# Mixture of experts: weights of the first experts loaded ahead into room that is free until later

## What is computed

```
x = x + 0.5 * ffn(layernorm(x))
x = x + attn(layernorm(x))
x = x + 0.5 * ffn(layernorm(x))

def ffn(h):                                 # E = 64 experts, 2 of them for each token
    x = rmsnorm(h) * rms_w
    topk_w, topk_ids = top_k(softmax(x @ gate_w.T), 2)
    xb = up to 256 of the tokens that chose expert e, for each e
    g, u = split(xb @ w13[e])               # w13[e]: 256 x 256 (256 KB)
    yb = (silu(g) * u) @ w2[e]              # w2[e]: 128 x 256 (128 KB)
    return weighted sum of a token's two yb rows + shared expert + h
```

## Time and profile before

| | us |
|---|---|
| median of three runs | 2201.7 (2197.7 to 2204.65) |
| the profiled execution | 2191.9 |
| its span, first to last instruction | 2189.4 |

### The profile page before, as it was taken

How to read it: one execution, slowest core, us unless ns; L and a number is a source line. 1 busy time by engine, 2 the same in 40 slices (tenths; PEclk the granted TensorE clock), 3 DMA queues, 4 the chain that set the end, 5 groups by cost and what they waited for, 6 DMA issues and landing times.

```text
span 2189.4 us, 32445 instructions
## 1 busy us (share of the span) xinstructions
PE 1970.7 (90%) x11044; PEld 1670.2 (76%) x11044; DVE 1310.7 (60%) x3467; ACT 1087.5 (50%) x1988; POOL 1116.0 (51%) x1252
## 2 busy tenths in 40 slices
PE   6996989499999999999999999999999973988887
PEld 4665888478888888888888888888888862888754
DVE  5995565445566566575576575575565452554467
ACT  6873666344445345444454454454454432555643
POOL 6785676444254555545545645645625325665500
PEclk9998999799999999999999999999999985999999
DMA  8434888790032032032031110110100202888778
GB/s 277 157 115 152 270 285 282 253 287 20 1 97 78 20 96 78 20 97 68 30 96 38 60 51 25 41 43 17 58 10 20 87 17 67 286 274 290 238 253 278
DMA packets 236407, 270.07 MB, mean 123 GB/s; under 512 B 25490, under 2 KB 186323, under 8 KB 236243
## 3 DMA queue, kind: packets, MB, share of 16 engines
q1 hardware_dynamic: 199122, 192.40, 27.4%
q0 software_dynamic: 28672, 67.22, 9.4%
q10 hardware_dynamic: 8448, 8.39, 1.1%
HBM read 150.35 MB, written 117.57 MB: 122 GB/s over the span
## 4 chain that ended last, share of the span: by engine, by line
PE 59%; DVE 8%; issue 5%; ACT 4%; POOL 2%; another core or an unknown queue 1%; DMA 1%; SPq 0%; ACTq 0%; DVEq 0%; POOLq 0%
PE attention_ring L1925 20%; PE attention_acc L1955 13%; PE attention_acc L1945 8%; DVE attention_hid_l L1658 2%; PE attention_work L1998 2%; PE attention_work L2031 2%; PE attention_work L2035 2%; PE attention_work L2015 2%; PE attention_acc L2138 2%; PE attention_ring L2164 2%; PE attention_acc L2128 1%; PE attention_work L1913 1%; PE attention_ring L2128 1%; PE attention_work L1972 1%
## 5 line engine op out<-in xcount | busy, mean ns | idle before, releaser
L1658 DVE TENSOR_TENSOR attention_hid_l<-attention_gelu,attention_hid_h 128x512 fp32r<-128x512 f32 x384 | 284.8, 742 | 495.4 <-ACT attention_gelu L1302 311.8
L1299 ACT ACTIVATE attention_hid_h<-attention_ring,home_b 128x512 fp32r<-128x512 f32 x384 | 264.2, 688 | 565.2 <-PE attention_ring L1925 488.8
L1302 ACT ACTIVATE attention_gelu<-attention_ring,home_b 128x512 f32<-128x512 f32 x384 | 261.7, 681 | 0.0
L1955 PE MATMUL attention_acc<-attention_hid_h,home_w_h 128*128 128x512 f32 x512 | 202.6, 396 | 20.8 <-DVE home_room L1684 18.0
L1925 PE MATMUL attention_ring<-attention_n_t_h,home_w_h 128*128 128x512 f32 x512 | 204.8, 400 | 1.4 <-DVE attention_n_t_l L1650 1.4
L1925 PE MATMUL attention_ring<-attention_n_t_h,home_w_l 128*128 128x512 f32 x512 | 200.6, 392 | 0.0
L1925 PE MATMUL attention_ring<-attention_n_t_l,home_w_h 128*128 128x512 f32 x512 | 200.2, 391 | 0.0
L1955 PE MATMUL attention_acc<-attention_hid_l,home_w_h 128*128 128x512 f32 x512 | 199.5, 390 | 0.0
L1955 PE MATMUL attention_acc<-attention_hid_h,home_w_l 128*128 128x512 f32 x512 | 199.4, 389 | 0.0
L1146 POOL DMA_INDIRECT home_room<-expert_rows,routing_slots x128 | 138.0, 1078 | 96.9 <-issue 52.7
L647 POOL DMA_INDIRECT experts_xg<-xn_rows,routing_affine x128 | 142.6, 1114 | 67.9 <-issue 35.2
(11 more groups left out here) (279 smaller groups left out, 5233.5 us busy)
## 6 DMA issues: line engine op xcount, KB each, us to landing
experts_w<-in_L_ffn_w SPq DMA_DIRECT2D x64, 256.0 KB
expert_rows<-experts_y SPq DMA_DIRECT2D x64, 256.0 KB
slot_rows<-const_zeros SPq DMA_DIRECT2D x16, 1024.0 KB
token_rows<-const_zeros SPq DMA_DIRECT2D x16, 1024.0 KB
home_room<-in_L_ffn_w SPq DMA_DIRECT2D x64, 256.0 KB
home_room<-slot_rows SPq DMA_DIRECT2D x64, 256.0 KB
final_y_rows<-token_rows SPq DMA_DIRECT2D x32, 512.0 KB, 6.7
dispatch_x_in<-in_L_attn_x SPq DMA_DIRECT2D x16, 512.0 KB, 6.5
```

Of the source, the lines that this page charges most:

```text
L1299: act.activation(hid[n % PARTS][0][:, :], ring[n % RING][:, :], ACT.Gelu, bias=b1[:, m, c:c + 1])
L1302: act.activation(gelu[n % GELUS][:, :], ring[n % RING][:, :], ACT.Gelu, bias=b1[:, m, c:c + 1]).then_inc(ring_free, 1)
L1658: dve.tensor_tensor(hid[n % PARTS][1][:, :], gelu[n % GELUS][:, :], hid[n % PARTS][0][:, :].bitcast(fp32), ALU.subtract).then_inc(hid_read ...
L1955: last = pe.matmul(acc[e % 3][:, :], w2[m][wp][:, c, k * P:(k + 1) * P], hid[s][xp][:, :], start=(c == 0 and q == 0), stop=(c == FC - 1 an ...
```

## The change

The weights of the first ten experts (FIRST = 10) go to tiles of their own, `home.first_w13` and `home.first_w2`, which lie over the last four of the twelve split attention weights (`h2_w2` and `fm_w2`, made after experts 31 and 47). For this the split weights get a fixed place at the upper end of SBUF, also during the dispatch. They are loaded in the dispatch by two DMAs (2.6 MB and 1.3 MB), which SP issues after `store_xn(10)` and so ahead of `store_base(8)`; nothing in the dispatch waits for them.

In the experts, SP first loads experts 10 to 13 into the ring. Experts 14 to 23 go again to the room of the first ten, in two lots of five (`load_again`, one DMA of 1.3 MB and one of 0.66 MB each), issued after the stores of experts 4 and 9. Experts 24 to 27 go to the ring one by one at e = 14, 16, 18 and 20, and from e = 24 on expert e + 4 is loaded as before. An expert's `w13` and `w2` share one semaphore now, and both `round_weights` and `down` wait until both have landed (`weights_in`); before, `round_weights` waited for `w13` alone.

```diff
                 store_xn(g)
                 if g + RX < GROUPS:
                     load_x(g + RX)
+                if g == GROUPS - RX:
+                    home.load_first(sp, w)
                 if g >= 2:
                     store_base(g - 2)
...
-        w13_loaded = [sem(f"w13_loaded{s}") for s in range(R)]
-        w2_loaded = [sem(f"w2_loaded{s}") for s in range(R)]
+        w_loaded, again_loaded = [sem(f"w_loaded{s}") for s in range(R)], [sem(f"again_loaded{n}") for n in range(2)]
...
+        FIRST, HALF = home.FIRST, home.FIRST // 2
+        AHEAD = FIRST + R
+        RING_AGAIN = AHEAD + FIRST
+        def held(e):
+            return e < FIRST or AHEAD <= e < RING_AGAIN
+        def slot_of(e):
+            return e % AHEAD if held(e) else (e - FIRST if e < AHEAD else e - RING_AGAIN) % R
+        def weights_in(e):
+            if e < FIRST:
+                return home.first_loaded, 32
+            if held(e):
+                return again_loaded[(e - AHEAD) // HALF], 32
+            return w_loaded[slot_of(e)], 32 * (1 if e < AHEAD else 2 + (e - RING_AGAIN) // R)
...
+            def load_again(n):
+                first, at = AHEAD + n * HALF, slice(n * HALF, (n + 1) * HALF)
+                sp.wait_ge(w_split, (n + 1) * HALF)
+                sp.dma_start(home.first_w13[:, at, :], w["w13"][first:first + HALF, :, :].rearrange("e (p k) f -> p e (k f)", k=KD)).then_inc(again_loaded[n], 16)
+                sp.wait_ge(y_ready, (n + 1) * HALF)
+                sp.dma_start(home.first_w2[:, at, :], w["w2"][first:first + HALF, :, :].rearrange("e p d -> p e d")).then_inc(again_loaded[n], 16)
...
-            for e in range(R):
+            for e in range(FIRST, AHEAD):
                 load_w13(e)
                 load_w2(e)
...
             for e in range(EXPERTS):
-                if e + R < EXPERTS:
+                if e in (HALF, 2 * HALF):
+                    load_again(e // HALF - 1)
+                if AHEAD <= e < AHEAD + 2 * R and e % 2 == 0:
+                    load_w13(RING_AGAIN + (e - AHEAD) // 2)
+                    load_w2(RING_AGAIN + (e - AHEAD) // 2)
+                if e >= RING_AGAIN and e + R < EXPERTS:
                     load_w13(e + R)
                     load_w2(e + R)
                 store(e)
...
             def round_weights(e):
-                act.wait_ge(w13_loaded[e % R], 16 * (e // R + 1))
+                act.wait_ge(*weights_in(e))
...
             def down(e):
                 pe.wait_ge(hidden_ready, e + 1)
-                pe.wait_ge(w2_loaded[e % R], 16 * (e // R + 1))
+                pe.wait_ge(*weights_in(e))
```

More of the change, by code:

```diff
@@ L654, in round_weights @@
             def round_weights(e):
[L655 removed]
+                act.wait_ge(*weights_in(e))
                 if e >= F:
                     act.wait_ge(gate_up_ready, e - F + 1)
[L658 removed]
+                act.activation(w13_hi[e % F][:, :, :], w13_of(e), ACT.Copy).then_inc(w_rounded, 1)
             def round_rows(e):
@@ L702, in split_weights @@
                     dve.wait_ge(gate_up_ready, e - F + 1)
-                dve.tensor_tensor(w13_lo[e % F][:, :, :], w13[e % R][:, :, :], w13_hi[e % F][:, :, :].bitcast(fp32), ALU.subtract).then_inc(w_split, 1)
+                dve.tensor_tensor(w13_lo[e % F][:, :, :], w13_of(e), w13_hi[e % F][:, :, :].bitcast(fp32), ALU.subtract).then_inc(w_split, 1)
             def split_rows(e):
@@ L762, in down @@
                 for c in range(CH):
-                    last = pe.matmul(ps_y[e % F][:, c, :], hidden[e % F][:, c * P:(c + 1) * P], w2[e % R][:, :], start=True, stop=True)
+                    last = pe.matmul(ps_y[e % F][:, c, :], hidden[e % F][:, c * P:(c + 1) * P], w2_of(e), start=True, stop=True)
                 last.then_inc(y_ready, 1)
@@ L806, in load, with load_first @@
             sp.dma_start(row[:, :], w[name].partition_broadcast(P)).then_inc(self.b_loaded, 16)
+    def load_first(self, sp, w):
+        sp.dma_start(self.first_w13[:, :, :], w["w13"][0:self.FIRST, :, :].rearrange("e (p k) f -> p e (k f)", k=KD)).then_inc(self.first_loaded, 16)
+        sp.dma_start(self.first_w2[:, :, :], w["w2"][0:self.FIRST, :, :].rearrange("e p d -> p e d")).then_inc(self.first_loaded, 16)
     def make_weights(self):
-        fr = mybir.dt.float32r
-        self.weights_at = -(-self.kit.nc.sbuf_base // 32) * 32
-        self.w1 = [[self.kit.sb(f"w1_{m}_{part}", [P, KD, 1024], fr) for part in "hl"] for m in range(3)]
-        self.w2 = [[self.kit.sb(f"w2_{m}_{part}", [P, 1024 // P, D], fr) for part in "hl"] for m in range(3)]
+        fr, at, size = mybir.dt.float32r, self.weights_at, 8192
+        place = self.kit.nc.alloc_sbuf_tensor_at
+        self.w1 = [[place(f"w1_{m}_{part}", [P, KD, 1024], fr, offset=at + (2 * m + n) * size) for n, part in enumerate("hl")] for m in range(3)]
+        self.w2 = [[place(f"w2_{m}_{part}", [P, 1024 // P, D], fr, offset=at + (6 + 2 * m + n) * size) for n, part in enumerate("hl")] for m in range(3)]
     def part(self, n, p):
```

22 lines of the change are left out of this document (15 added, 7 removed).

## The result

| | before | after |
|---|---|---|
| median of five runs, us | 2201.7 (2197.7 to 2204.65) | 2214.2 (2212.1 to 2221.2) |
| the profiled execution, us | 2191.9 | 2212.1 |
| its span, us | 2189.4 | 2209.9 |

The ratio is 1.006, 95% interval 1.0042 to 1.0078: slower by 13 us. The two profiled executions lie 20 us apart: the one of before was 9.8 us faster than its median, the one of after 2.1 us, so some 8 of the 20 are chance.

A forecast was written before the change was run, and what follows sets the result against it. PE's own work was taken to bound the experts, DMA close behind. 0 - 0.5 + 0 + 2 + 0.3 = +1.8 us on 2191.9 gave 2193.7; with the median's 9.8, 2203.5, stated as 2203; range 2190 to 2217.

The forecast's parts named there:

- ACT's first rounding: Sign at the start of the experts: if the forecast is right, ACT rounds the first weights before 191 us.
- the longer and more frequent waits of ACT: Sign after expert 28: more ACT waits on loads than 8, near 0.5 us longer.
- PE's first transposition: Sign at the experts' start: 6 to 7 us after POOL's first gather; before 196 would show the forecast wrong.
- Fixed places in SBUF: Whole kernel: fixed places and fewer semaphores change no instruction, cost 0.
- The joint wait: Experts from 28 on: rounding also waits for w2; 8 waits, 0.5 us each, half absorbed: +2, bounds 0 and +18.
- the lottery of plus or minus 5: Experts: the clock's falls after PE's six stalls vary by chance, 5.2 us lost may be 0 or twice that.
- Experts up to 23: Experts before 24: ACT's waits for weights go, 2.6 us in 4 times; -0.5 us, between 0 and -4.
- DMA is the bound after all: Rival in the experts: 3.93 MB fewer to load there gives -14 us, 2188; chance 0.13.
- The start: Start of the experts: PE still waits for the first gathered rows, cost 0; bounds -3 and +0.5 us.
- The two lots: Loads behind stores of experts 4 and 9: later stores keep a 2.5 us margin, cost 0, +6 at most.
- The dispatch: Early load delays group 8's base, normalise(13) 2 to 3 us late, 3.6 us cover: +0.3, bounds 0 and +2.
- the rival of the joint wait: Rival in the experts: late w2 delays ACT's copy of y and next loads; +9 to +18 us, chance 0.17.

The follow-up runs named there:

- experiment 2: Kernel after with separate semaphores for w13 and w2 in the ring, so rounding waits for w13 alone: 2209.6 us, 1.0028 of before.
- 4: Kernel before with split attention weights moved by 32 bytes and the tiles behind them by 64: 2212.8 us, 1.0042 of before.
- 6: Kernel after with only the split attention weights moved to byte 130048, a multiple of 1024; joint wait kept: 2204.2 us, 0.9993 of before.
- experiment 5: Kernel after with split weights at byte 130048 and separate waits for w13 and w2, leaving early loads and lots: 2201.6 us, 0.9984 of before.
- 7: Kernel before with one edit, w13 and w2 sharing a semaphore so rounding waits for both: 2209.8 us, 1.0023 of before.
- experiment 1: Kernel after with split attention weights starting at byte 131008, a multiple of 64, instead of 131040: 2215.3 us, 1.0043 of before.
- 3: Kernel after with split weights at byte 131008 and separate waits for w13 and w2: 2207.8 us, 1.0013 of before.
- 8: Kernel before with split attention weights moved by 64 bytes and everything behind them by 128: 2204.5 us, 1.0006 of before.
- experiment 9: Kernel before without the weight loads of experts 4 to 63 (23.6 MB), which reuse weights of experts 0 to 3: 0.9933 of before, 14.3 us less.
- experiment 10: Version of experiment 5 with loads of experts 10 to 13 issued behind the stores of experts 0 to 3: 0.9988 of before.
- experiments 9 to 12: The third chip's runs; the one without its own line, 11, is the kernel before with weights moved 128 bytes, tiles behind 256: 1.0047 of before.
- experiment 12: Kernel before with a 64-byte pad behind the split weights, which stay while the other tiles move by 64: 0.9984 of before.

## Why the prediction was right or wrong

The forecast was +1.8 us and the measured loss some 13. The result lies in the range, but by luck: its largest term is one that the prediction put at 0. Measured by its own band of 0.3% around no change, what came is "slower", to which it gave 0.24. Of its signs, ACT's first rounding (189.91), the end of the dispatch and the longer and more frequent waits of ACT came as said; PE's first transposition came 7.5 us behind the gather and not 6 to 7, and PE waited for `w13_lo` 10 times and not six.

- **Fixed places in SBUF, 0**: this is the step that failed, and the term was the largest of all. It changed no instruction, but the pace of nearly all matmuls of the attention. By the traces +11 to +12 us (experiments 2 and 4 and the kernel after alike); by the ratios 0.0067, 15 us (after against 6), and 0.0044, 10 us (2 against 5). The step looked for what the change does to instructions and left out what it does to operands; start addresses can be read from the code, but nothing in the trace of before priced them.
- **The joint wait, +2, bounds 0 and 18**: the mechanism was right (more and longer waits of ACT on loads from expert 28 on, 13 for 8), the size too small. By the ratios it is 2 us (6 against 5), 5 us (7), 6 to 7 us (1 against 3; after against 2). By the traces it is some 5 us: from the 25th `gate_up` to the last, the four kernels with the joint wait on the first two chips took 130.1 to 133.6 us (7: 130.1, 6: 130.3, 1: 132.5, after: 133.6), the six without it 124.8 to 127.1 (before: 124.8, 8: 125.3, 2: 125.5, 3: 126.9, 4: 127.0, 5: 127.1). What was mis-sized is the share that reaches PE: half of eight roundings, 0.5 us each, was counted. In the kernel after, one delay also came together with an attention part and with a longer fall of the clock. The stall behind the part after expert 39 in the kernel after:

```profile
344.12 0.58 PE L791 MATMUL experts_ps_gu<-experts_x_hi,experts_w_hi 128*128 128x256 f32 x1 [3.09 <-DVE experts_w_lo L741]
```

and in the kernel before:

```profile
341.88 0.39 PE L753 MATMUL experts_ps_gu<-experts_x_hi,experts_w_hi 128*128 128x256 f32 x1 [1.94 <-DVE experts_w_lo L703]
```

The stretch from 340 to 352 us, columns as in the earlier trace rows, after:

```profile
340.00:352.00 12.00, 8.91 (x44) 8.11 (x43) 7.00 (x10) 6.38 (x13) 6.04 (x5) 0.72 0.65 210
```

and before:

```profile
340.00:352.00 12.00, 10.12 (x61) 9.46 (x62) 6.77 (x12) 6.17 (x14) 8.86 (x8) 0.86 0.84 266
```

A stall of 3.09 us instead of 1.94, and a clock of 0.72 instead of 0.86. Over the experts the clock was at half for 20.4 us in five falls, and for 10.2 us in three before; at half speed about half of it is lost, so by this estimate 5 of the 6.7 us at the last `gate_up` are clock. How much of that is the joint wait's doing isn't shown: behind the 25th `gate_up` experiments 6 and 7 have two falls each, experiment 5, without the joint wait, has three, and yet 6 and 7 take some 3 us longer there. The falls are the lottery of plus or minus 5 that the prediction named, and this execution drew badly.
- **Experts up to 23, -0.5, bounds -4 and 0**: -2.6, inside its bounds, and the sign right. Some 1.7 of it is one fall of the clock fewer (one instead of two before the 25th `gate_up`), so the trace alone would prove little. On the first two chips the six kernels with the early loads took 69.8 to 72.3 us from the third `gate_up` to the 25th, the four without them 72.1 to 74.7. The argument that no wait of PE names a load was too strong. Experiment 9 shows what a load costs without ever being named: a late load is a late `w13_lo`, and the name in PE's wait is DVE's. The rival that DMA is the bound after all falls nevertheless: -14 us was its price for 3.93 MB, and that is what 23.6 MB bring.
- **The start, 0**: right (third `gate_up` +0.5). Its lower bound of -3 was real, too: experiment 10 finds 2.3 us there, by taking away the four loads that the change left.
- **The two lots, 0**: right. No wait of ACT on a store shows, and PE does as much in the 15 us behind each lot's issue (224.8 and 242.9) as before. Stretches of the kernel after, then of the kernel before, columns as in the earlier trace rows:

```profile
225.00:240.00 15.00, 12.47 (x79) 11.32 (x78) 9.34 (x14) 9.70 (x18) 10.14 (x9) 0.91 0.91 305
245.00:260.00 15.00, 14.63 (x104) 13.88 (x104) 8.55 (x16) 10.83 (x21) 10.69 (x10) 1.00 0.96 325
...
225.00:240.00 15.00, 12.25 (x75) 11.32 (x76) 9.41 (x15) 9.48 (x18) 10.56 (x9) 0.91 0.89 287
245.00:260.00 15.00, 14.60 (x105) 13.86 (x104) 8.46 (x16) 10.65 (x21) 9.70 (x11) 1.00 0.91 297
```

 PE did 79 and 104 instructions there instead of 75 and 105, and waited for no gather; strict order of arrival would have cost it up to 7 us for each lot. When a lot landed (13.9 us was worked out) is not in the trace. The Trainium skill (DMA: Bandwidth & Descriptors, Queues, rings and completion order) has each DMA engine alternate between its queues; by that rule, the trace agrees.
- **The dispatch, +0.3**: right in each step: 2.4 us late at `normalise(13)` (2 to 3 worked out), 0.08 left at DVE. The load itself was slower than the 13.8 us worked out: issued from 118.1 on, it had landed at 133.8, 15.7 us or 250 GB/s, which is the rate of the upper bound of +2. The cover held even so.

The sum was +1.8 us against some +13; the range held it by way of the rival of the joint wait (+9 to +18), which stands for at most half of it. A right range with the main cause missing is luck.

## What to carry to other kernels

A tile that is given a fixed place in SBUF is a change to every instruction that reads it: compare its start address, by its remainder, with the one before, and look at the step from one matmul to the next in an untouched stage before looking for a cause in the edited one. When an edit runs out of a resource (semaphores here) and merges two waits, price the merged wait through everything that is queued behind it, to the engine that sets the pace. And a wait names the last link of a chain: to price a transfer, take it away, as experiment 9 did.

## What the runs showed of the hardware

- The start addresses of stationary and moving operand change the step of a 512-column float32r matmul from 227 to 229, 232 or 234 ns and that of a 256-column one from 120 to 118, 117 or 114 ns, at the full granted clock. What rule is behind it stays open.
- From the third `gate_up` to 1715 us, every fall of the clock from 2.4 to 1.2 GHz (1.00 to 0.50 granted) came within 1.5 us behind a stall of PE of 1.7 us or more, or during one (one more falls in PE's 27 us wait at the start of the attention, in all runs). Not every stall of that length had one behind it: one of 3.28 us in experiment 2 had none. No shorter one had. So a closer spacing of matmuls can be waited away. Against the kernel after, the steps of experiment 1 are shorter by some 14 us between 520 and 1700 us (3.9 and 5.1 ns in the two 512-column lines, 2.4 ns in L1993), and the ratio is lower by 0.0017 only, 4 us; by estimate the rest went into five falls of 1.6 us and into 4.5 us more in PE's 13 waits for DVE (22.4 and 17.9). In 3 and 8, with five and three falls, the time can't be told from that of the kernel before.
- On the third chip the 13 waits of PE for DVE in the attention are absent (in experiments 9 to 12 one or two stalls above 1.2 us between 425 and 1715 us, fourteen in the profile of the kernel before), no clock falls between these times once the one at the start of the attention is over, and the closer spacing of experiment 12 was kept.
- The kernel before took 2202 and 2204 us on two chips and 2137 on the third. The 227 ns between matmuls are the same there (experiments 9 and 10); the DMA engines moved 292 and 291 GB/s in two stretches of the experts (experiment 12), against 269 and 281 in the earlier trace rows, and the stalls of the attention are gone. Why isn't shown.
